# Which engine forms the low half of the attention output: a subtraction moved from VectorE to GpSimd

## The reference

```python
B, N, C = x.shape                      # 2, 8192, 512
q, k, v = split(layernorm(x) @ w_qkv)  # 16 heads of 32
# local: blocks of 64 queries against three blocks of 64 keys, inside a window of 64
attn_local = softmax(where(valid, q_block @ k_near.T * scale, NEG))
out_local = attn_local @ v_near
# global: every query against every 64th key
attn_g = softmax(q @ k[:, ::64].T * scale)
out_global = attn_g @ v[:, ::64]
x = x + layernorm((out_local + out_global) @ w_out + b_out)
# spectral block: fft, a sparse complex matrix, inverse fft, real part, + bias
x = x + layernorm(spectral(layernorm(x)))
```

## Time and profile before

| | |
|---|---|
| runs shown | 4066.57, 4060.76, 4060.36 us; median 4060.76 |
| the profiled execution's own time | 4062.74 us |
| its span, first to last instruction | 4060.1 us |
| mean granted TensorE clock | 0.978 of full speed |
| busy over the span: PE, DVE, POOL, ACT | 94%, 61%, 42%, 40% |
| attention phase | from about 1,400 us to the end; one chunk takes about 80.6 us |

### The profile page before, as it was taken

The page is one execution under the profiler, slowest core; times in us unless marked ns, Lnnn a source line. Parts: engine busy times, 40 slices in busy tenths (PEclk is TensorE's granted clock), DMA queues, the critical chain, the costliest instruction groups (busy, mean ns, idle before and its releaser), DMA issues.

```text
span 4060.1 us, 77910 instructions
## 1 busy us (share of the span) xinstructions
PE 3813.0 (94%) x28864; PEld 2734.1 (67%) x28864; DVE 2489.9 (61%) x5844; ACT 1616.0 (40%) x3094; POOL 1710.5 (42%) x2574
## 2 busy tenths in 40 slices
PE   5999999999996589999999999999999999999997
PEld 4777777777773256666666666666666666666665
DVE  3333333333330357777777777777877777777775
ACT  2222222222220034554555445545555555555553
POOL 0000000000000036666666666666666666666665
PEclk9999999999998789999999999999999999999999
DMA  4445445444534366656665665566556655665651
GB/s 131 149 165 186 161 149 186 175 146 175 186 141 159 68 130 138 139 132 140 147 139 133 140 147 135 133 144 146 132 134 144 144 133 133 147 141 133 138 122 37
DMA packets 415894, 574.44 MB, mean 141 GB/s; under 512 B 38585, under 2 KB 179145, under 8 KB 415577
## 3 DMA queue, kind: packets, MB, share of 16 engines
q1 hardware_dynamic: 413176, 568.00, 53.6%
q10 hardware_dynamic: 2112, 2.15, 0.2%
q0 software_dynamic: 288, 0.08, 0.0%
HBM read 364.81 MB, written 203.23 MB: 140 GB/s over the span
## 4 chain that ended last, share of the span: by engine, by line
PE 56%; ACT 4%; ACTq 3%; issue 2%; DVE 1%; DMA 0%; POOL 0%; SPq 0%; POOLq 0%; DVEq 0%
PE ps_misc L931 17%; PE ps_max L849 10%; PE ps_sc L871 6%; PE ps_max L852 4%; PE ps_o L903 4%; PE ps_o L915 3%; PE ps_s L909 3%; PE ps_sc L885 3%; PE ps_s L903 3%; ACTq L704 3%; ACT p_glob L694 1%; PE ps_sc L940 1%; ACT y_buf L672 1%; ACT mt L700 1%; PE ps_sc L859 1%
## 5 line engine op out<-in xcount | busy, mean ns | idle before, releaser
L757 DVE TENSOR_REDUCE mx<-ps_max 128x2 f32<-128x256 f32 (+1 forms) x1365 | 482.2, 353 | 441.0 <-PE ps_max L852 434.3
L681 ACT ACTIVATE p_loc<-ps_sc 128x384 f32<-128x384 f32 (+1 forms) x1024 | 431.5, 463 | 619.1 <-PE ps_sc L871 611.8
L624 POOL TENSOR_SCALAR_AFFINE_SELECT p_loc<-p_loc 128x512 f32<-128x512 f32 (+1 forms) x512 | 309.4, 604 | 792.4 <-ACT p_loc L681 788.5
L849 PE MATMUL ps_max<-ks,qs 97*128 97x384 f32 x2048 | 586.0, 366 | 45.0 <-DMA ks<-bias_d 37.0
L758 DVE TENSOR_REDUCE mx<-ps_max 128x2 f32<-128x384 f32 (+1 forms) x1365 | 611.2, 448 | 0.0
L849 PEld LDWEIGHTS ps_max<-ks,qs 97*128 97x128 f32 x2048 | 352.2, 191 | 333.6 <-DVE mx L758 236.6
L291 DVE TENSOR_TENSOR o_lo<-po,o_hi 128x512 fp32r<-128x512 f32 x256 | 177.1, 692 | 536.5 <-ACT o_hi L235 536.5
L326 PE MATMUL po<-ht_hi,w_hi 128*128 128x512 f32 x1024 | 416.7, 407 | 65.8 <-DVE ht_lo L269 59.9
L694 ACT ACTIVATE p_glob<-ps_sc 128x512 f32<-128x512 f32 x512 | 306.3, 598 | 419.4 <-PE ps_o L915 227.2
L206 POOL CAST kg_hi<-o_hi 128x32 f32 (+1 forms) x32 | 7.4, 233 | 959.7 <-DVE o_lo L291 959.7
L326 PE MATMUL po<-ht_lo,w_hi 128*128 128x512 f32 x1024 | 407.7, 398 | 0.0
(11 more groups left out here) (114 smaller groups left out, 7845.1 us busy)
## 6 DMA issues: line engine op xcount, KB each, us to landing
ks<-k_hi_d SPq DMA_DIRECT2D x256, 288.0 KB
qs<-q_hi_d SPq DMA_DIRECT2D x256, 256.0 KB
ks<-k_lo_d SPq DMA_DIRECT2D x128, 288.0 KB
xb<-in_L_attn_x SPq DMA_DIRECT2D x32, 1024.0 KB, 13.3
q_hi_d<-o_hi SPq DMA_DIRECT2D x32, 1024.0 KB, 4.3
k_hi_d<-o_hi SPq DMA_DIRECT2D x32, 1024.0 KB, 6.4
q_lo_d<-o_lo SPq DMA_DIRECT2D x32, 1024.0 KB, 8.7
k_lo_d<-o_lo SPq DMA_DIRECT2D x32, 1024.0 KB, 10.2
```

The source lines that it names most:

```text
L681: nc.scalar.activation(p_loc[:, i, 2 * hp:2 * hp + 2, lo:MW], ps_sc[n % 2][:, 0:2 * MW].rearrange("p (h n) -> p h n", h=2)[:, :, lo:MW], A ...
L757: nc.vector.tensor_reduce(mx[s % 2][:, tile, 1, h:h + n], ps_max[:, b:b + n, MW:MW + NGLOB], axis=AX.X, op=ALU.max)
L849: nc.tensor.matmul(ps_max[:, b, 0:2 * MW], qs[g][0:ROWS_MAX, h, tile * P:(tile + 1) * P], both_keys(g, h, tile), start=True, stop=True)
```

## The change

GpSimd issues the subtraction `ot_lo = o_loc - ot_hi` in place of VectorE. It does so where its own walk through the list comes to `otl`, behind the same wait for `ot_hi` (`oth_done`), and increments the same semaphore. Nothing else is edited.

```diff
@@ gpsimd @@
                         pool.wait_ge(ol_done, s + 1)
                         pool.tensor_tensor(o_loc[s % 2][:], o_loc[s % 2][:], o_glob[:], ALU.add).then_inc(o_sum, 1)
+                    if name == "otl":
+                        pool.wait_ge(oth_done, s + 1)
+                        pool.tensor_tensor(ot_lo[:, s % GROUPS, :], o_loc[s % 2][:], ot_hi[:, s % GROUPS, :].bitcast(F32),
+                                           ALU.subtract).then_inc(otl_done, 1)
                     n = s * TILES + i + 1
@@ vector @@
                         nc.vector.tensor_tensor(o_glob[:], ps_o[:], r_glob[:], ALU.mult).then_inc(og_done, 1)
-                    if name == "otl":
-                        dve.wait_ge(oth_done, s + 1)
-                        nc.vector.tensor_tensor(ot_lo[:, s % GROUPS, :], o_loc[s % 2][:], ot_hi[:, s % GROUPS, :].bitcast(F32),
-                                                ALU.subtract).then_inc(otl_done, 1)
                     n = s * TILES + i + 1
```

## The result

The changed kernel takes 4234.02 us (median of 4 runs, 4231.36 to 4235.16) against 4061.37 for the one before (4 runs). The ratio is 1.0421, 95% interval 1.0403 to 1.044: 171 to 173 us slower, of which the forecast had 153. The profiled execution took 4234.43, its span is 4232.4.

The account below looks back on a forecast made before the run. TensorE, busy 2375.78 of 2400 us, was taken to set the attention phase's pace. 108.5 + 2.8 + 42 = 153.3 us on the profiled 4062.7 gave 4216.0, so 4214 as median; range 4172 to 4240 us.

Parts of the forecast that it names:

- The chain, 3.5 us: Group 3, chunks 0 to 30: `out` waits for scores, exponentials, two selects and the subtraction, 3.5 us each, 108.5 us.
- The subtraction's price, 1.28: One subtraction on GpSimd takes 1.28 us, from an addition of the same shape; bounds 0.68 to 1.71.
- The last chunk, 2.8: Last chunk's `out`: a residual addition and a normalization's two scalar operations stand ahead of the subtraction, 2.8 us later.
- Groups 0 to 2 at nothing: The subtractions of groups 0, 1 and 2 are covered on GpSimd: cost 0, at most 123 us.
- VectorE's relief at 0 to 3 us: 128 subtractions leave VectorE's stream: gain between nothing and 24 us, taken as 0 to 3.
- The clock, 42 us: TensorE's granted clock drops behind 28 of 31 new gaps, 1.5 us each: 42 us, bounds 15 to 53.
- a case of its own: Rival: low clock lasts over two stretches, or covers of groups 0 to 2 partly fail: 4245 to 4275 us, chance 0.09.
- the main case's own range: Stall plus clock drops, chance 0.74: 4061 + 94 + 31 x 1.0 = 4186 to 4061 + 124 + 53 = 4238 us.
- The one without drops: Rival: the stall comes without most of the clock's drops, 4172 to 4187 us, chance 0.13.
- The one on the other side: Rival: VectorE's relief outweighs the stall, all 24.2 us of TensorE's idle time go, end near 4035; chance 0.02.
- The signs: Profile after: `out` waits 31 times or more, about 3.5 us; clock 0.50 behind most stalls; VectorE lower by over 88 us.

Follow-up runs that it names:

- the filled version: The changed kernel with 14 matmuls that do no work for the result on TensorE ahead of the wait of `out`, chunks 0 to 30: 4175.33 us, ratio 1.0276.
- the early place: The changed kernel with group 3's subtraction on GpSimd ahead of a normalization's scalars and tile 1's masks (planned time 15.75, not 16.73): 4058.9 us, ratio 0.9987.
- the early versions: Group 3's subtraction earlier, against the kernel before: all subtractions on VectorE 4056.73 us, group 3 alone on GpSimd 4059.92, all on GpSimd 4058.9, again 4059.57.
- the version on VectorE: The kernel before, all subtractions on VectorE, group 3's one place earlier, ahead of a maxima reduction (planned time 16.05): 4056.73 us, ratio 0.9982.
- the early version: The changed kernel, all subtractions on GpSimd, group 3's at planned time 15.75 in place of 16.73: 4058.9 us, ratio 0.9987; again 4059.57, ratio 0.9989.
- 7 filling matmuls: The changed kernel with 7 instead of 14 matmuls that do no work for the result ahead of the wait of `out`: 4212.05 us, ratio 1.0373.
- the versions with gaps of 1.63 to 2.24 us: The changed kernel, group 3's subtraction just ahead of tile 1's masks: 4125.18 us (gap 1.63); or behind the exponentials' wait, ahead of the selects: 4156.94 us (2.24).

## Why the prediction held, and where it was short

**The chain, 3.5 us.** Shown. The rows after have every link within 0.02 us of the length taken from the rows before, the wait of 115.5 us in 32 times is 31 x 3.54 and the last chunk's 5.87, and the filled version puts the stall at ratio 1.0276, 112 us, where the sum had 108.5 + 2.8 = 111.3.

**The subtraction's price, 1.28.** Shown, 1.279 in the median. The rule of the Trainium skill (GPSIMD Engine Reference, When to use GPSIMD) that such work is about 2x slower there agrees roughly: 1.279 against 0.686, a factor of 1.9. But that factor is not what cost the time. At the early place the same 1.28 us cost nothing.

**The last chunk, 2.8.** Shown. The timeline of GpSimd, after, in which the addition takes 1.26 where it took 1.71:

```profile
4177.92 1.26 POOL L657 TENSOR_TENSOR y_buf<-y_buf,x_res 128x512 f32<-128x512 f32 x1
4179.15 0.55 POOL L615 TENSOR_TENSOR rsb<-veb,mhalf_b 128x1 f32<-128x1 f32 x1
4179.79 0.26 POOL L617 TENSOR_SCALAR nmb<-mvb,rsb 128x1 f32<-128x1 f32 x1
4180.01 1.26 POOL L642 TENSOR_TENSOR ot_lo<-o_loc,ot_hi 128x512 fp32r<-128x512 f32 x1
```

And TensorE's first piece of that `out`:

```profile
4181.42 0.77 PE L931 MATMUL ps_misc<-wo_hi,ot_hi 128*128 128x512 f32 x1 [5.87 <-POOL ot_lo L642]
```

TensorE's gap there went from 3.08 to 5.87 us.

**Groups 0 to 2 at nothing.** Shown: 0.9999.

**VectorE's relief at 0 to 3 us.** Shown for groups 0 to 2 by the same run. The 0.1 to 0.2% that the early versions gain are not relief, since they come with VectorE doing all the work too. They follow the place of group 3's subtraction: the version on VectorE differs from the kernel before in nothing else. That it is the wait of `out` in the earlier trace rows, 0.2 us a chunk or 6 us, fits the size; no trace isolates it.

**The clock, 42 us.** The mechanism is shown by the filled version: without the idle time no drops, and the loss shrinks by a third. This is the term of the sum that was mis-sized: 59 us, the difference of the two ratios times 4061. I took a drop behind 28 of 31 gaps at 1.5 us each. It came behind all 31, and 11 of the low stretches lasted 6.8 us in place of 3.4, which I had put among the rivals as a case of its own. Per drop 59 / 31 = 1.9 us. These 17 us are nearly all of the 20 between forecast and result, and they put the result only 6 us under the upper end of the range. Two numbers of the main case's own range don't come out of the working: its lower end takes 94 for the stall, where 90 + 2.8 is 92.8, and 31 for the clock, where the bounds had 15.

**The rivals.** The one without drops (4172 to 4187) is what the filled version shows. The one on the other side, relief over stall with an end near 4035, had as its condition that GpSimd reaches the subtraction ahead of the selects. In the early version it does, and the time is 4058.9. So relief isn't worth 24 us without the stall either. The reading behind that bound, that TensorE's idle time is a wait for VectorE's maxima, was wrong. In the kernel before, from 1600 to 3930 us, the only wait of matmuls for another engine is for ScalarE (us in all, times, longest):

```profile
PE ps_sc L871 <- ACT p_glob L694: 20.0, 88, 0.5
```

In the early version it is 19.8 us. Only weight loads wait for the maxima (209.8 us from 1600 us to 4000, in both versions), beside matmuls that go on.

**The signs.** The wait of `out`, GpSimd's order without idle time between the second select and the subtraction, and the low stretches are as described. VectorE is busy for 2380.7 us in place of 2489.9, 109 less (forecast: over 88), and a chunk takes about 86.0 us (forecast: 85.5). ScalarE waited once for the subtraction, 1.5 us, where the forecast had never.

## What to carry to other kernels

When an operation changes its engine in a hand-written order, its place has to be set anew: the planned time that was set for the old engine says nothing about what stands ahead of it on the new one. Look for the pair "consumer just behind, and something just ahead that depends on the consumer's own engine"; the bound engine then waits for a whole round trip, here TensorE, ScalarE, GpSimd and back, 3.5 us for an operation that is 0.6 us slower. And price the idle time of a bound TensorE twice, once as itself and once for the clock behind it: here 112 and 59 us.

## What the runs showed of the hardware

The drop of TensorE's clock is not a simple matter of the gap's length. A gap of 1.63 us was followed by a low stretch 7 times in 30, one of 2.24 us 16 times in 31, but one of 1.79 us, behind 7 filling matmuls, 25 times in 31, and one of 0.76 us never. The kernel before has the like in its projection phase, where 12 of 31 gaps of about 2.1 us were followed by one. The drops are not scattered: behind the gaps of 2.24 us they came at every second chunk exactly, and behind those of 1.79 us they stayed away at every fourth to sixth. That points to the moment at which a gap falls as well as to its length. It is not shown; no run here was made for it.

The double length goes with the moment too: the 11 stretches of 6.8 us had all begun inside the gap (above), and in the versions with gaps of 1.63 to 2.24 us, where every low stretch of chunks 0 to 30 began behind the start of `out`, all lasted 3.4.

A VectorE subtraction with both inputs in SBUF, beside a GpSimd addition, took 1.60 us in place of 0.68, and a GpSimd operation beside it 1.00 in place of 0.55. In the version with groups 0 to 2 on GpSimd, the 32 subtractions left on VectorE took 1.60 in the median (its group among those that write `ot_lo`):

```profile
L785 DVE TENSOR_TENSOR ot_lo<-o_loc,ot_hi x32: 681/1604/1612, 1528.0 to 4013.5; 128x512 fp32r<-128x512 f32 x32
```

This agrees with the rule of the Trainium skill (SBUF — State Buffer, Who interferes with whom) on which the prediction drew. Having less of it was worth nothing measurable here. Before, group 0's subtractions were lengthened too (1.38 us in the median); with groups 0 to 2 on GpSimd they are off VectorE, and the ratio is 0.9999. The early version with all work on GpSimd has none of it left and is no faster than the one with all work on VectorE.
